# x turned in blocks by VectorE instead of by TensorE, queries ahead of keys, and the adapters' first product between them

## The reference

```python
def layer0(x, W, A, Bm, scalings, idx):         # dense, with an adapter per sequence (8 of rank 16)
    H = einsum('btd,od->bto', x, W)
    xa = einsum('btd,brd->btr', x, A[idx])
    return H + einsum('btr,bor->bto', xa, Bm[idx]) * scalings[idx][:, None, None]
def layer1(x, cond, weights):                   # mixes the tokens of a sequence by a 64 x 64 table row
    return einsum('bct,bcd->bdt', x, weights[cond])
def layer2(x, precision, Wq, Wk, Wv, Wo):       # attention in a sequence, 16 heads of 32
    q = proj(x, Wq) * minimum(precision, 4.0)
    scores = einsum('bhqd,bhkd->bhqk', q, proj(x, Wk)) / sqrt(32)    # causal
    out = einsum('bhqk,bhkd->bhqd', softmax(scores), proj(x, Wv))
    return einsum('bsd,ed->bse', out, Wo)
# layer3 is layer1 with another table
x = x + layer0(x, ...); x = x + layer1(x, ...); x = x + layer2(x, ...); x = x + layer3(x, ...)
```

## Time and profile before

| | us |
|---|---|
| median of 3 runs (669.57 to 670.38) | 669.94 |
| the profiled execution | 668.29 |
| its span, first to last instruction | 666.5 |
| TensorE busy | 637.4 |
| VectorE busy | 351.7 |
| ScalarE busy | 225.6 |
| GpSimd busy | 140.6 |

### The profile page before, as it was taken

The page is one execution under the profiler, slowest core; times in us unless marked ns, Lnnn a source line. Parts: engine busy times, 40 slices in busy tenths (PEclk is TensorE's granted clock), DMA queues, the critical chain, the costliest instruction groups (busy, mean ns, idle before and its releaser), DMA issues.

```text
span 666.5 us, 19636 instructions
## 1 busy us (share of the span) xinstructions
PE 637.4 (96%) x7800; PEld 542.4 (81%) x7800; DVE 351.7 (53%) x526; ACT 225.6 (34%) x440; POOL 140.6 (21%) x113
## 2 busy tenths in 40 slices
PE   4689999999999999999999999999999999999985
PEld 4568787988889798888879888887979889797864
DVE  3445664464745446474544647454464745445372
ACT  3533343223343323334332333433233343322221
POOL 1003213040311304031230403122040312204040
PEclk9989999999999999999999999999999999999999
DMA  7611200203030020302012020300203030100101
GB/s 261 210 31 41 61 6 21 77 0 91 3 87 8 22 73 0 92 3 88 7 23 71 1 91 2 88 7 24 71 2 90 2 88 7 36 26 1 38 1 64
DMA packets 29514, 31.90 MB, mean 48 GB/s; under 512 B 15278, under 2 KB 15278, under 8 KB 29486
## 3 DMA queue, kind: packets, MB, share of 16 engines
q1 hardware_dynamic: 25390, 25.22, 13.2%
q10 hardware_dynamic: 4096, 6.29, 2.8%
HBM read 22.58 MB, written 8.91 MB: 47 GB/s over the span
## 4 chain that ended last, share of the span: by engine, by line
PE 91%; DMA 3%; DVE 2%; SPq 2%; issue 1%; ACT 1%; POOL 0%; ACTq 0%; DVEq 0%
PE banks L444 10%; PE banks L449 9%; PE banks L445 9%; PE banks L421 5%; PE banks L470 5%; PE banks L527 5%; PE banks L532 4%; PE banks L498 4%; PE banks L528 4%; PE banks L474 4%; PE banks L472 4%; PE banks L398 4%; PE banks L400 4%; PE banks L396 4%; PE banks L488 3%; PE banks L513 3%
## 5 line engine op out<-in xcount | busy, mean ns | idle before, releaser
L444 PE MATMUL banks<-x1T_hi,w_hi 128*128 128x256 f32 x512 | 130.3, 287 | 0.7 <-ACT x1T_hi L640 0.7
L1010 POOL TENSOR_TENSOR probs<-probs,row_max 128x1024 f32<-128x1024 f32 x32 | 61.0, 1907 | 323.3 <-DVE row_max L872 323.3
L445 PE MATMUL banks<-x1T_hi,w_lo 128*128 128x256 f32 x512 | 128.1, 283 | 0.0
L444 PEld LDWEIGHTS banks<-x1T_hi,w_hi 128*128 128x128 f32 x512 | 97.9, 191 | 2.3 <-ACT x1T_hi L640 1.0
L445 PEld LDWEIGHTS banks<-x1T_hi,w_lo 128*128 128x128 f32 x512 | 98.0, 191 | 0.0
L449 PE MATMUL banks<-x1T_lo,w_hi 128*128 128x256 f32 x512 | 82.4, 283 | 0.0
L449 PEld LDWEIGHTS banks<-x1T_lo,w_hi 128*128 128x128 f32 x512 | 70.6, 192 | 0.1
L858 DVE TENSOR_TENSOR qkT<-banks,beta 128x512 f32<-128x512 f32 x32 | 22.1, 692 | 66.6 <-PE banks L449 66.6
L470 PE MATMUL banks<-w_hi,x1T_hi 128*128 128x512 f32 x128 | 51.6, 403 | 1.5 <-issue 0.3
L876 DVE TENSOR_REDUCE row_sum<-probs 128x16 f32<-128x1024 f32 x32 | 39.1, 1221 | 25.7 <-ACT probs L711 25.7
L527 PE MATMUL banks<-w_hi,attnT_hi 128*128 128x512 f32 x128 | 50.6, 396 | 0.9 <-DVE attnT_hi L799 0.9
(11 more groups left out here) (93 smaller groups left out, 1149.2 us busy)
## 6 DMA issues: line engine op xcount, KB each, us to landing
out_dram<-x_y SPq DMA_DIRECT2D x16, 512.0 KB, 3.1
x_in<-in_x_dram SPq DMA_DIRECT2D x15, 512.0 KB, 4.2
b_sel<-b_parts SPq DMA_DIRECT2D x192, 32.0 KB, 1.7
w_in<-in_L_cond_weights_dram SPq DMA_DIRECT2D x128, 16.0 KB
probsT<-in_L_cond_W_dram ACTq DMA_DIRECT2D x1, 1024.0 KB, 9.1
probs<-in_L_cond_Wk_dram ACTq DMA_DIRECT2D x1, 1024.0 KB, 11.2
x_both<-in_L_cond_Wq_dram ACTq DMA_DIRECT2D x1, 1024.0 KB, 13.6
probsT<-in_L_cond_Wv_dram ACTq DMA_DIRECT2D x1, 1024.0 KB, 6.3
```

Source lines behind the costliest of these rows:

```text
L444: nc.tensor.matmul(out_ap, w_hi[:, w, c, cols], x1T_hi[:, c, :], start=(c == 0), stop=False)
L445: nc.tensor.matmul(out_ap, w_lo[:, w, c, cols], x1T_hi[:, c, :], start=False, stop=False)
L1010: nc.gpsimd.tensor_tensor(heads(probs[:, g, :]), heads(probs[:, g, :]), rows[:, g, :].unsqueeze(2).to_broadcast([P, HEADS, S]), op).then_i ...
```

## The change

1. x of a pair is loaded in four transfers, each into 32 partitions: 32 tokens of each half sequence on the partitions and a quarter of the features in rows of 128 numbers. VectorE turns it in one instruction, in blocks of 32 x 32 (STREAM_TRANSPOSE), into a new tile `xT` in SBUF. It reads every fourth feature, so that chunk c of the turned x holds the features 4p + c on partition p. W, A and B are turned to the same order of features (`every_fourth`, `ordered`). ScalarE and VectorE make `xT_hi` and `xT_lo` from `xT`, one instruction each in place of two. Only x of pair 0 is still turned by TensorE.
2. The queries are projected ahead of the keys, `adapters_down(i + 2)` stands between them, and `scores` waits for the second half of the keys only in its middle.
3. Of the second half of the probabilities one transposition stands ahead of `layer1` and seven behind it; the last transposition of x1 stands behind the wait for the copied probabilities and y. ScalarE and VectorE copy x1 before the second half of the probabilities, and each copies one tile of y.
4. Ahead of the loop: W is loaded first, by SP. The identity is added to it in SBUF by GpSimd, not in PSUM by VectorE. `b_parts` is stored before the rows of w1 are gathered, and x of pair 1 is loaded after the rows of B. `select_a(1)` comes behind x's high part.

```diff
+X1T, Q = SC[0:2], SC[2:4]
+SQ = 32
+BLOCKS = PT // SQ
+    x_blocks = x.rearrange("(i q) (h j) (g n) -> i g j (q h) n", q=PSEQ, j=SQ, g=JG)
-        x_in = sb("x_in", [P, TILES, D])
+        x_in = sb("x_in", [P, BLOCKS, P])
+        xT = sb("xT", [P, NC, PT])
+        def every_fourth(ap, c):
+            return ap.rearrange("q (p c) -> q c p", c=NC)[:, c, :]
             def load_x(i):
-                sp.dma_start(x_in[:], x_v[i] if isinstance(i, int)
-                             else x_v[bass.ds(i, 1)].rearrange("a p t d -> (a p) t d")).then_inc(x_loaded, 16)
+                for g in range(JG):
+                    sp.dma_start(x_in[g * SQ:(g + 1) * SQ], x_blocks[i, g] if isinstance(i, int)
+                                 else x_blocks[bass.ds(i, 1), g].rearrange("a j b n -> (a j) b n"))\
+                        .then_inc(x_loaded, 16)
...
             for part, b_part in enumerate((b_hi, b_lo)):
                 sp.dma_start(b_parts[part], b_part[:].bitcast(F32)).then_inc(b_parts_stored, 16)
-            sp.wait_ge(xT_mm, TILES)
-            load_x(1)
+            gather(w1_in, w1, w1_of_pair0, w1_loaded, False)
             sp.wait_ge(b_parts_stored, 16 * 2)
             gather_b(adapters_of_pair0)
+            load_x(1)
...
             def scores(i):
                 pe.wait_ge(k_copied_act, i + 1)
-                pe.wait_ge(k_copied_dve, i + 1)
                 pe.wait_ge(q_scaled, TILES * (i + 1))
                 for mm in range(NC // 2):
+                    if mm == 1:
+                        pe.wait_ge(k_copied_dve, i + 1)
...
+                pe.wait_ge(probs_done[1], i + 1)
+                turn_probs(i, 1, range(1))
                 if nxt:
                     layer1()
-                if nxt2:
+                turn_probs(i, 1, range(1, 8))
+                if nxt:
                     pT_copied(i, 1)
-                    turn_x(i + 2)
-                pT_copied(i, HG)
-                if nxt:
-                    turn_x1(i + 1, 0)
+                    pe.wait_ge(x1_copied_act, i + 2)
+                    turn_x1(i + 1, 0, range(NC))
+                    pe.wait_ge(x1_copied_dve, i + 2)
+                    turn_x1(i + 1, 1, range(NC - 1))
                 if prev:
-                    pe.wait_ge(y_copied, TILES * i)
+                    pe.wait_ge(y_copied_act, i)
+                    pe.wait_ge(y_copied_dve, i)
                 else:
                     pe.wait_ge(v_copied, TILES)
-                if nxt:
-                    turn_x1(i + 1, 1)
+                pT_copied(i, HG)
+                if nxt:
+                    turn_x1(i + 1, 1, range(NC - 1, NC))
                 attend()
...
+            def x_hi(i):
+                act.wait_ge(x_turned, i)
+                if not (isinstance(i, int) and i == 1):
+                    act.wait_ge(x0_mm, TILES * i)
+                copy(xT_hi[:], xT[:]).then_inc(xT_hi_done, 1)
...
+            def turn_x(i):
+                dve.wait_ge(x_loaded, 16 * JG * i)
+                nc.vector.transpose(xT[:].rearrange("p c (b j) -> p b c j", j=SQ),
+                                    x_in[:].rearrange("p b (e c) -> p b c e", c=NC)).then_inc(x_turned, 1)
+
             def x_lo(i):
-                for t in range(TILES):
-                    dve.wait_ge(xT_hi_done, TILES * i + t + 1)
-                    rest(xT_lo[:, :, tok(t)], in_chunks(bank[SC[t]]), xT_hi[:, :, tok(t)]).then_inc(xT_split, 1)
+                dve.wait_ge(xT_hi_done, i)
+                rest(xT_lo[:], xT[:], xT_hi[:]).then_inc(xT_split, 1)
...
                 if nxt2:
+                    turn_x(i + 2)
                     x_lo(i + 2)
...
+            pool.wait_ge(w_loaded[W0], 16)
+            nc.gpsimd.tensor_tensor(diagonal, diagonal, ident[:].unsqueeze(1).to_broadcast([P, NC, P]), ALU.add)\
+                .then_inc(diag_added, 1)
```

More of the change, by code:

```diff
@@ L357, in _, with turn @@
         def _(pe):
-            def turn(g, pieces):
+            def turn(g, pieces, ordered=None):
                 before = [n for n in range(g) if ring[n] == ring[g]]
@@ L744, in step @@
                 if nxt2:
[L745 removed]
+                    x_hi(i + 2)
                 if nxt:
                     if not prev:
[L748 to L751 removed]
+                        for c in range(2):
                             take_hi(GROUPS_OF[WO][c], w_hi[:, WO, c, :])
@@ L755, in step @@
                         xa_hi_part(i + 2)
+                    if not prev:
+                        for c in range(2, NC):
+                            take_hi(GROUPS_OF[WO][c], w_hi[:, WO, c, :])
+                    copy_k(i + 1)
             def take_matrix(k):
@@ L919, in step @@
                         for c in range(2):
-                            take_lo(GROUPS_OF[WO][c], w_lo[:, WO, c, :], w_hi[:, WO, c, :])
-                    copy_k(i + 1)
-                    if not prev:
-                        for c in range(2, NC):
                             take_lo(GROUPS_OF[WO][c], w_lo[:, WO, c, :], w_hi[:, WO, c, :])
@@ L929, in step @@
                         xa_lo_part(i + 2)
+                    if not prev:
+                        for c in range(2, NC):
+                            take_lo(GROUPS_OF[WO][c], w_lo[:, WO, c, :], w_hi[:, WO, c, :])
+                    copy_k(i + 1)
             def take_matrix(k):
@@ L960, in _ @@
             xa_lo_part(0)
-            take_matrix(WQ)
-            x_lo(1)
+            for c in range(2, NC):
+                take_lo(GROUPS_OF[WQ][c], w_lo[:, WQ, c, :], w_hi[:, WQ, c, :])
             x0_copy(0)
@@ L978, in _ @@
             x1T_lo_part(0)
-            for c in range(2, NC):
-                take_lo(GROUPS_OF[WV][c], w_lo[:, WV, c, :], w_hi[:, WV, c, :])
-            copy_k(0)
+            take_lo(GROUPS_OF[WV][3], w_lo[:, WV, 3, :], w_hi[:, WV, 3, :])
+            turn_x(1)
+            x_lo(1)
             scale_q(0)
```

228 lines of the change are left out of this document (117 added, 111 removed).

## The result

The change makes the kernel **slower by 1.04%**: 676.23 us (674.18 to 680.06, 4 runs) against 669.76 us (669.05 to 670.38, 4 runs), ratio 1.0104 with a 95% interval of 1.0057 to 1.0150. The forecast was 658.0 us, and its range ended at 670.0. The profiled execution took 674.18 us (span 672.4 us), 5.89 more than that of before.

A forecast was written before the change was run, and what follows sets the result against it. TensorE was taken as the bound, busy 637.4 of 666.5 us. Savings of 8.2 + 1.5 - 0.4 + 2.2 + 0.45 = 11.95 us took the profiled 668.29 to 656.3; adding 1.65 for the median gave 658.0, range 655.5 to 670.0.

The forecast's parts named there:

- The price of the turning, d: Duration of VectorE's turning of x in each step: taken as 1.22 us, with 2.07 kept as the other end.
- first rival: Turning slow by its 16-byte read step, 2.07 us: TensorE waits 0.65 a step, time 667.9 us; chance 0.22.
- second rival: VectorE turns four-byte elements in two passes, 2.44 us or more: 3.6 us lost, 673.5 us; chance 0.14.
- Before attention: From the second half of the turned probabilities to attention: 3.94 us becomes 3.11, saving 0.83 us a step.
- Rival 3: Hand-overs a tenth dearer before attention or in scores, or d of 1.5 to 1.9: 662.5 to 667 us; chance 0.14.
- The wait: TensorE's wait for x's low part at the adapters' first product: none below 1.42 us of turning, 0.65 at 2.07.
- Scores: Scores after the keys: nothing covers VectorE's copy of the keys' second half, 0.20 us lost a step.
- Step 0: First loop step: 1.1 us more waiting for Wo's pieces, 0.2 in scores, 0.9 saved; a loss of 0.4 us.
- Ahead of the loop: Start of the kernel: B's rows 3.6 us earlier, 2.3 lost waiting for selected A, 0.9 at first scores; 2.2 gained.
- Step 14 and the tail: Step 14 gains 1.5 us, half before attention and half in scores; the last copies of y side by side save 0.45.

The follow-up runs named there:

- both cures: Changed kernel with the adapters' first product behind the keys again and x loaded in 128-byte rows, so the turning reads in order: 661.36 us, ratio 0.9877.
- all three edits: Changed kernel with the adapters' first product behind the keys, x in 128-byte rows in natural order, and W loaded by ScalarE's queue: 659.85 us, ratio 0.9866.

## Why the prediction was wrong

**The step that failed is "The price of the turning, d"**: "I take 1.22, the row with the same size, memory and order of writing, and keep 2.07 as the other end." The turning took 2.068 us, to 0.002 the end that was worked out from the two operations which write at that step. (VectorE's one, the 1114 ns row, also reads `b_hi` at it, which the prediction didn't say; none reads so without writing so.) I had put more weight on how an operation writes than on the step of its addresses. In order it takes 1.235, so the 1.22 was the price of another access. The rest of that path nearly stood: the three hand-overs took 0.29 us together where 0.20 was counted (7.27 less 3.36, 1.06, 1.22 and 1.34), VectorE begins the turning at attention + 3.36 (434.73 less 431.37), ScalarE's high part took 1.06, VectorE's low part 1.22.

**The rest of the miss** is as large, and in sizes. With x read in order, so with the price that I took, the kernel still needs 667.1 us, 9.1 more than the forecast of 658.0, and only just beats the kernel before. With d at the far end the prediction said 667.9 us, its first rival; 676.23 were measured. Of the 7.9 us between that rival and the profiled execution, 4.7 lie in the twelve steps, 1.8 ahead of attention of step 0 and 0.9 in step 0. The second rival's 673.5 us is nearer to the result, but its mechanism, two passes for each element, is what reading in order excludes.

- *Before attention.* Forecast 0.83 saved, measured 0.56 (3.94 to 3.38). The times of the copies came to the hundredth: the last transposition begins 2.82 after layer 1 (431.14 less 428.32), as forecast. But a transposition by itself between products takes 0.26 (427.99 to 428.25) where 0.17 was counted, and the last one, which waits, 0.30 where 0.12 was counted. Together 0.27 a step. Rival 3 had this mechanism, at a tenth.
- *The wait.* Forecast 0.65 at d = 2.07, measured 0.73 and 0.06 for the restart.
- *Scores.* Forecast 0.20 lost, measured 0.17 (the step with the product at the end against the one with it between, both without a wait).
- So the step: -0.56 + 0.17 + 0.79 = +0.40, and 39.20 - 38.80 is 0.40. Without the last two it is -0.56: 38.24, measured for the product at the end.
- *Step 0.* The estimate of 1.1 us for the pieces of Wo behind the adapters' chain was half of what it cost: TensorE waits 2.2 us in one go for the low part of a piece, and 0.6 before that for another, which stood behind the turning (with x read in order this wait is gone). Both, between attention of step 0 and of step 1:

```profile
PE banks L385 <- DVE w_lo L832: 2.8, 2, 2.2
```

- *Ahead of the loop.* The store of B's parts went as forecast. For W at the head of the other queue I had counted "perhaps 0.5" for the small tables behind it, and nothing for what it takes from x and B on ScalarE's queue: x landed 2.7 us and B 7.9 us later. Of the 3.6 us, 1.74 were left, and the wait for selected A, 2.1 us, ate them. (The forecast's 2.3 was for d = 1.22; with x read in order it is 1.2.)
- *Step 14 and the tail.* -0.71 for -0.75; -0.22 for -0.45.

What was right: that TensorE's work counts in full until another engine is late; who would be late; where it waits; the seven transpositions as cover (0.58 us a step when they are gone). The sign was wrong because the gain of the step, 0.63 us forecast and 0.39 real, was smaller than the 0.79 us that one mispriced instruction cost.

## What to carry to other kernels

A new instruction on the engine that has time is still priced twice: its own duration, and the slack of who waits for it. Work both out; where the price has two ends and the slack lies between them, as here (1.22, 2.07, and 1.34), the place of the waiting instruction can be the cheaper thing to change: moved one projection back, the slack was 5.8 us wider and the price no longer mattered. Look at the byte step of every operand, of reads as of writes. And a split of TensorE's work into single instructions costs some 0.1 to 0.2 us for each piece that stands alone or waits.

## What the runs showed of the hardware

**The step of the read.** A transposition by VectorE, 128 x 1024 elements of four bytes, SBUF to SBUF: 1.235 to 1.239 us in the mean when it reads in order, 2.063 to 2.068 when successive reads are 16 bytes apart. Single ones, 15 in each profile, took 1.233 to 1.242 and 2.059 to 2.089.

**A stop of 1.8 to 2.2 us.** In eight of the thirteen profiled executions TensorE stops once in the attention of step 14, with no releaser in the profile. The profiled execution of the changed kernel has no stop, its repetition has one. TensorE in order of time, the changed kernel once more:

```profile
626.33 1.23 PE L536 MATMUL banks<-probsT,v 64*32 64x64 f32 x103
629.73 0.43 PE L536 MATMUL banks<-probsT,v 64*32 64x64 f32 x25 [2.18 <-issue]
```

Behind such a stop the granted clock was lower in three of the eight, as here with the product last (busy time by engine; 0.66 is the share of full clock):

```profile
610.00:615.00 5.00, 2.91 (x139) 2.30 (x137) 2.16 (x4) 1.77 (x3) 0.00 (x0) 1.00 0.31 108
615.00:620.00 5.00, 5.00 (x33) 5.00 (x30) 2.28 (x4) 0.60 (x1) 0.00 (x0) 0.66 0.04 10
```

Attention 14 to attention 15 takes 31.1 to 31.8 us without a stop and 33.1 to 34.9 with one, so the stop and its clock are 2 to 4 us. They don't explain by themselves why runs of one kernel scatter by several us: the profiled executions of the kernel with both cures (657.58 us) and with all three edits (657.51) have the stop and are the fastest of their five. The traces have a candidate for the cause. In all eight a packet of 16 KB on the queue that the page calls "instruction" starts 0.0 to 0.5 us before the stop (in the changed kernel once more at 627.07, the stop is from 627.56 to 629.73). In the five others it starts more than 3 us ahead of that attention (in the changed kernel at 623.78, attention at 627.02) or, in the kernel before, behind it. So TensorE may have stood there waiting for its own instructions; no run tried it. A stretch cut out of the middle of the loop is free of the stop, which is why the steps tell these kernels apart where the medians hardly do.

**The clock behind a wait.** With x read in order, the granted clock from 90 to 95 us was 0.75, a mean of its two levels, 1.2 and 2.4 GHz, after TensorE had been busy for 2.78 of the 5 us before (its wait of 2.2 us in step 0). In the changed kernel the same wait, with TensorE busy for 2.77 of those 5 us, left the clock at 1.00, so the wait alone doesn't decide it. With x read in order the lower clock took more than the faster turning gave in step 0: attention 0 to 1 takes 44.08 us, where the changed kernel takes 43.20. The columns are those of the earlier trace rows, and the last line is of the changed kernel:

```profile
85.00:90.00 5.00, 2.78 (x21) 2.58 (x20) 1.95 (x4) 3.41 (x9) 0.00 (x0) 0.91 0.06 13
90.00:95.00 5.00, 5.00 (x146) 4.67 (x145) 0.97 (x2) 1.00 (x4) 0.00 (x0) 0.75 0.04 10
```

```profile
90.00:95.00 5.00, 5.00 (x156) 4.79 (x156) 1.38 (x2) 2.33 (x6) 0.00 (x0) 1.00 0.08 16
```
